# Low half of the embedding summed once and kept on both row halves: keys, queries and values with half-row products, tokens a step later

## What is computed

```
h = einsum('bnk,dk->bnd', patches(x), W)
q, k, v = silu(h @ Wq), silu(h @ Wk), silu(h @ Wv)        # 12 heads of 16
out = einsum(einsum(q, k) * decay, v) * sigmoid(h @ Wg1 @ Wg2)
h = layernorm(h + layernorm(out @ Wo) * ln_w + ln_b)
logits = l2(slots) * scale . l2(rms_norm(h)) ; dispatch, combine = softmax over tokens, over slots
y = fc2(gelu(fc1(xn . dispatch) + b1)) + b2 ; h = layernorm(h + y . combine)
```

## Time and profile before

| | |
|---|---|
| median of 3 runs | 1220.85 us (1219.61 to 1221.07) |
| profiled execution | 1220.71 us |
| its span, first to last instruction | 1219.0 us |
| mean granted TensorE clock over the span | 0.958 |
| busy, share of the span: TensorE, VectorE, ScalarE, GpSimd | 91%, 65%, 62%, 49% |

### The profile page before, as it was taken

The page is one execution under the profiler, slowest core; times in us unless marked ns, Lnnn a source line. Parts: engine busy times, 40 slices in busy tenths (PEclk is TensorE's granted clock), DMA queues, the critical chain, the costliest instruction groups (busy, mean ns, idle before and its releaser), DMA issues.

```text
span 1219.0 us, 35974 instructions
## 1 busy us (share of the span) xinstructions
PE 1105.5 (91%) x13418; PEld 889.2 (73%) x13418; DVE 787.8 (65%) x2082; ACT 750.0 (62%) x1745; POOL 595.9 (49%) x942
## 2 busy tenths in 40 slices
PE   4899999999999999999999999999998999997563
PEld 3787888888888888888888888788886556564332
DVE  5577766677777777676777777777774222222996
ACT  5567677777777776777777777776763111110676
POOL 3366655565555666555655555665533000000664
PEclk9999999999999999999999999999999999998555
DMA  4411121111111111211111111112063999995786
GB/s 151 197 51 55 58 84 59 62 53 53 53 53 53 53 53 55 80 66 61 55 53 53 53 53 53 53 53 77 32 263 129 368 424 423 424 423 181 235 264 183
DMA packets 50718, 158.41 MB, mean 130 GB/s; under 512 B 5386, under 2 KB 31392, under 8 KB 38372
## 3 DMA queue, kind: packets, MB, share of 16 engines
q1 hardware_dynamic: 33080, 145.09, 32.2%
q10 hardware_dynamic: 17600, 12.78, 3.4%
HBM read 132.23 MB, written 25.62 MB: 129 GB/s over the span
## 4 chain that ended last, share of the span: by engine, by line
PE 71%; DVE 22%; issue 2%; ACT 1%; DVEq 1%; SPq 1%; DMA 1%; POOL 0%; ACTq 0%; POOLq 0%
DVE p_sb L828 9%; PE ps L974 8%; PE ps L976 7%; PE ps L975 7%; PE ps L1271 6%; PE ps L1052 5%; PE ps L1089 4%; PE ps L1290 4%; PE ps L1134 4%; DVE gn L803 3%; PE ps L1031 3%; PE ps L1032 3%; PE ps L1019 2%; PE ps L1157 2%; DVE res L943 2%
## 5 line engine op out<-in xcount | busy, mean ns | idle before, releaser
L427 POOL TENSOR_TENSOR xl<-x_sb,xh 128x392 fp32r<-128x392 f32 x192 | 189.8, 1026 | 84.1 <-DVE gn L803 74.9
L828 DVE TENSOR_TENSOR p_sb<-ps,dec 98x1568 f32<-98x1568 f32 x96 | 171.6, 1788 | 14.8 <-PE ps L1052 14.8
L678 ACT ACTIVATE hg<-ps 128x768 f32<-128x768 f32 x32 | 25.9, 810 | 146.0 <-PE ps L1295 146.0
L768 DVE BATCH_NORM_STATS2 st<-ps 98x6 f32<-98x192 f32 x128 | 40.0, 354 | 77.5 <-PE ps L1019 77.5
L935 DVE COPY y2st<-ps 128x192 f32<-128x192 f32 x32 | 11.4, 358 | 120.5 <-PE ps L1271 120.5
L695 ACT ACTIVATE o_sb<-res,nb,rstd 98x192 f32<-98x192 f32 x128 | 59.5, 535 | 44.8 <-DVE nb L958 44.1
L1089 PE MATMUL ps<-p_sb,vpad 98*32 98x98 f32 x3072 | 84.9, 250 | 1.6 <-DVE p_sb L828 1.6
L1319 PE MATMUL ps<-y2b,cbuf 64*98 64x192 f32 x256 | 49.3, 537 | 38.1 <-POOL y2b L532 38.1
L1089 PEld LDWEIGHTS ps<-p_sb,vpad 98*32 98x32 f32 x3072 | 64.1, 109 | 26.7 <-issue 26.2
L519 POOL CAST pickb<-pick 128x128 fp32r (+1 forms) x32 | 9.4, 293 | 148.8 <-PE ps L1295 148.8
L974 PE MATMUL ps<-xl,wh 128*128 128x392 f32 x192 | 70.1, 365 | 13.1 <-POOL xl L427 13.1
(11 more groups left out here) (203 smaller groups left out, 3484.8 us busy)
## 6 DMA issues: line engine op xcount, KB each, us to landing
x_sb<-in_xT SPq DMA_DIRECT2D x32, 1176.0 KB, 5.2
w1v<-in_fc SPq DMA_DIRECT2D x32, 1152.0 KB, 10.2
w2v<-in_fc SPq DMA_DIRECT2D x32, 1152.0 KB, 12.7
h_dram<-h SPq DMA_DIRECT2D x32, 294.0 KB
h2r<-h_dram SPq DMA_DIRECT2D x32, 294.0 KB
out<-o_sb ACTq DMA_DIRECT2D x32, 294.0 KB
comb_dram<-cst SPq DMA_DIRECT2D x32, 98.0 KB, 1.7
cbuf<-comb_dram SPq DMA_DIRECT2D x32, 98.0 KB, 3.8
```

The lines of the kernel that those rows point to most:

```text
L427: pool.tensor_tensor(xl[:, k], x_sb[:, k], xh[:, k].bitcast(F32), ALU.subtract)\
L828: dve.tensor_tensor(dst, src, rate.unsqueeze(2).to_broadcast([T, 4, 2, TOK]), ALU.mult)\
```

## The change

The two partial sums of the last 64 features are added once. ScalarE copies the low part from partitions 64 to 127 into `kA[0:64]` (semaphore `hlo_sb`), VectorE adds it to the high part twice, into partitions 0 to 63 and 64 to 127 of `hT[:, 1]` (`summed_h`, `hx_rdy`), and ScalarE and VectorE make the high and low parts of that as before. The second contraction of queries, keys and values is then over 64 rows: `project` writes both output groups in turns, group 0 with rows 0 to 63 and group 1 with rows 64 to 127. Keys come first, in banks 2 and 3, then queries in banks 0 and 1; the values of the first image stand in banks 4 and 5, one half of the tokens on each row half; those of the second image in bank 7, all on rows 0 to 63. The turned embedding takes four matmuls of 64 rows instead of four of 128.

Around it the order changes on every engine. VectorE makes the tokens of pair i - 2 at the start of step i (before: of pair i - 1 in front of the first decay), the token norms between first norm and residual of the second tiles, the cosine scales behind the second statistics, the cosines in front of the `zs` subtraction, and the slots' maximum behind the second decay. ScalarE makes the squares in front of the new copy and into a buffer of their own, loads the SiLU table behind `hTh`, rounds the pixels in two places, and takes keys before queries. TensorE moves the gate behind the turned keys, the turned logits (now two transposes) in front of the third scores, and the last values in front of the slots' inputs. Output weights and slot rows are prepared at the end of step 0 instead of before it.

```diff
-V_AT = (2, 7)
+K_AT, Q_AT, V_AT = 2, 0, (4, 7)
...
-            sp.wait_ge(k_mm, 2)
+            sp.wait_ge(slT_sb, 1)
...
             def step(i, a, c, d, d_before, more):
-                if d:
-                    inverse_norms(i - 2)
...
+                if d:
+                    inverse_norms(i - 2)
...
                 if more:
-                    if c:
-                        pool.wait_ge(gn_rdy, 4 * i)
                     split_x(i + 1, range(KP))
+                if at_start(i):
...
+                if not (isinstance(j, int) and j == 0):
+                    pool.wait_ge(cosc_rdy, j)
...
+                pool.wait_ge(gn_rdy, 4 * j + 4)
...
-                if d:
+                if d and a:
                     second_norm(i - 2)
                 if a:
-                    turned_h(i, 0)
+                    turned_h(i)
                 if d:
                     act.wait_ge(tokT_mm, i - 1)
                     act.activation(tokT[:, :, :], ps[0:G, 6:8, 0:PT], ACT.Copy).then_inc(tokT_sb, 1)
-                if a:
+                    if a or c:
+                        squares(i - 2)
+                    if not a:
+                        second_norm(i - 2)
+                if a:
+                    act.wait_ge(hT_mm, 2 * i + 2)
+                    act.activation(kA[0:64, :], ps[64:128, 1, 0:PT], ACT.Copy).then_inc(hlo_sb, 1)
+                    act.wait_ge(hx_rdy, 2 * i + 2)
+                    act.activation(hTh[:, 1], hT[:, 1], ACT.Copy).then_inc(hTh_rdy, 1)
                     use_table(ACT.Silu)
-                    turned_h(i, 1)
-                if more:
-                    for k in range(2):
-                        round_x(i + 1, k)
-                if a:
+                    if more:
+                        round_x(i + 1, 0)
+                    act.wait_ge(k_mm, 2 * i + 1)
+                    act.activation(kA[:, :], ps[:, K_AT, 0:PT], ACT.Silu).then_inc(k_sb, 1)
+                    act.wait_ge(k_mm, 2 * i + 2)
...
                     act.wait_ge(q_mm, 2 * i + 1)
...
+                    act.wait_ge(v_mm, 2 * i + 1)
+                    act.activation(vpad[:, 0:2].rearrange("p t (j q d) -> p t j q d", q=4, d=HD)[:, :, :, 0:4:3, :],
...
                     act.wait_ge(q_mm, 2 * i + 2)
...
-                    act.wait_ge(k_mm, 2 * i + 1)
-                    act.activation(kA[:, :], ps[:, 0, 0:PT], ACT.Silu).then_inc(k_sb, 1)
-                    act.wait_ge(k_mm, 2 * i + 2)
...
+                    act.wait_ge(v_mm, 2 * i + 2)
+                    act.activation(vpad[:, 2:4].rearrange("p t (j q d) -> p (t j) q d", q=4, d=HD)[:, :, 0:4:3, :],
...
+                    if more:
+                        round_x(i + 1, 1)
                     if c:
                         act.wait_ge(og_sb, 2 * i)
                     act.wait_ge(g_mm, 2 * i + 1)
...
-                    turned_v(i, 1)
-                if c:
...
+                elif c:
+                    squares(i - 1)
                 if d:
                     use_table(ACT.Exp)
                     exponentials(i - 2)
...
+            def squares(j):
+                for t in range(4):
+                    act.wait_ge(gn_rdy, 4 * j + t + 1)
+                    act.activation(ysq[:, t], gn[0:T, t], ACT.Square, accum_out=ss[:, t:t + 1]).then_inc(ss_rdy, 1)
...
+            def mean_shifts(j):
+                dve.wait_ge(ra_rdy, j + 1)
...
+            def summed_h(i):
+                dve.wait_ge(hlo_sb, i + 1)
+                for x in range(2):
+                    dve.tensor_tensor(hT[64 * x:64 * x + 64, 1], ps[0:64, 1, 0:PT], kA[0:64, :],
+                                      ALU.add)                        .then_inc(hx_rdy, 1)
...
-                    token_norms(i - 2)
+                    mean_shifts(i - 2)
                 if c:
                     for g, n in enumerate((slice(0, PT), slice(PT, COLS))):
                         dve.wait_ge(ogh_rdy, 2 * i - 1 + g)
                         dve.tensor_tensor(ogl[:, n], og[:, n], ogh[:, n].bitcast(F32), ALU.subtract)\
                             .then_inc(ogl_rdy, 1)
+                if d and (a or c):
+                    tokens(i - 2)
+                if c:
                     first_norm(i - 1, 0)
                     residual(i - 1, 0)
+                if a:
+                    summed_h(i)
+                if c:
                     residual_statistics(i - 1, 0)
                 if a:
                     dve.wait_ge(hTh_rdy, 2 * i + 2)
...
                 if c:
                     first_norm(i - 1, 1)
                 if d:
-                    cosine_scales(i - 2)
+                    token_norms(i - 2)
                 if c:
                     residual(i - 1, 1)
                     residual_statistics(i - 1, 1)
+                if d:
+                    cosine_scales(i - 2)
                 if a:
                     if c:
                         dve.wait_ge(t2_rdy, 4 * i)
...
-                    dve.wait_ge(q_sb, 2 * i + 2)
-                    dve.tensor_tensor(zs[ZL:ZL + RANK, :], ps[DB:DB + RANK, 1, 0:PT], zs[0:RANK, :].bitcast(F32),
+                if d:
+                    cosines(i - 2)
+                if a:
+                    dve.wait_ge(zh_rdy, 2 * i + 2)
+                    dve.tensor_tensor(zs[ZL:ZL + RANK, :], ps[DB:DB + RANK, Q_AT + 1, 0:PT], zs[0:RANK, :].bitcast(F32),
                                       ALU.subtract).then_inc(zl_rdy, 1)
-                if d:
-                    cosines(i - 2)
-                if c:
+                if c and not a:
                     tokens(i - 1)
                 if d and not a:
                     slot_maxima(i - 2)
...
+                    decay(i, 1)
                     if d:
                         slot_maxima(i - 2)
-                    decay(i, 1)
                     dve.wait_ge(s_mm, i + 1)
...
                     sums(i - 2)
                 if a:
                     decay(i, 2)
+                    if at_start(i):
+                        output_weights()
                     gated(i, 0)
                     gated(i, 1)
+                    if at_start(i):
+                        slot_rows()
...
-            def project(i, g, hi, lo, done, more=0):
-
-                m = slice(0, DA) if g == 0 else slice(DA, D + more)
-                for k in range(2):
-                    pe.wait_ge(hTl_rdy[k], i + 1)
-                    mm = product(ps[0:m.stop - m.start, g, 0:PT], hi[:, k, m], lo[:, k, m], hTh[:, k], hTl[:, k],
-                                 k == 0, k == 1)
-                mm.then_inc(done, 1)
+            def project(i, bank, hi, lo, done, more=0):
+                groups = (slice(0, DA), slice(DA, D + more))
+                pe.wait_ge(hTl_rdy[0], i + 1)
+                for g, m in enumerate(groups):
+                    product(ps[0:m.stop - m.start, bank + g, 0:PT], hi[:, 0, m], lo[:, 0, m], hTh[:, 0], hTl[:, 0],
+                            True, False)
+                pe.wait_ge(hTl_rdy[1], i + 1)
+                for w, h in ((hi, hTl), (lo, hTh), (hi, hTh)):
+                    for g, m in enumerate(groups):
+                        rows = slice(64 * g, 64 * g + 64)
+                        mm = pe.matmul(ps[0:m.stop - m.start, bank + g, 0:PT], w[rows, 1, m], h[rows, 1],
+                                       start=False, stop=(w is hi and h is hTh))
+                        if w is hi and h is hTh:
+                            mm.then_inc(done, 1)
 
             def rows_of_v(i, a):
-                for t in (2 * a, 2 * a + 1):
-                    for k in range(2):
-                        n = slice(t * T, (t + 1) * T)
-                        mm = product(ps[0:T, V_AT[a], (t % 2) * D:(t % 2) * D + D],
-                                     hTh[:, k, n], hTl[:, k, n], wvh[:, k], wvl[:, k], k == 0, k == 1)
+                def at(mt):
+                    return ps[0:T, V_AT[0] + mt, 0:D] if a == 0 else ps[0:T, V_AT[1], mt * D:(mt + 1) * D]
+
+                def whole(mt):
+                    n = slice((2 * a + mt) * T, (2 * a + mt + 1) * T)
+                    product(at(mt), hTh[:, 0, n], hTl[:, 0, n], wvh[:, 0], wvl[:, 0], True, False)
+
+                def half(mt, h, w):
+                    x, n = mt if a == 0 else 0, (2 * a + mt) * T
+                    rows = slice(64 * x, 64 * x + 64)
+                    return pe.matmul(at(mt), h[rows, 1, n:n + T], w[rows, 1],
+                                     start=False, stop=(h is hTh and w is wvh))
+                pairs = ((hTh, wvl), (hTl, wvh), (hTh, wvh))
+                if a == 0:
+                    for mt in range(2):
+                        whole(mt)
+                    for h, w in pairs:
+                        for mt in range(2):
+                            mm = half(mt, h, w)
+                else:
+                    for mt in range(2):
+                        whole(mt)
+                        for h, w in pairs:
+                            mm = half(mt, h, w)
```

(80 more changed lines are left out.)

112 lines of the change are left out of this document (55 added, 57 removed).

## The result

The median is 1285.35 us (four runs, 1284.54 to 1286.91) against 1220.96 beside it: ratio 1.053, 95% interval 1.0512 to 1.0548, so +64.4 us. The profiled execution has a span of 1281.6 us.

The account below looks back on a forecast made before the run. TensorE was fullest (26.91 of 28 us a step), VectorE's chain nearly as long. VectorE's terms, 1.59 - 0.82 + 0.7 + 0.2 = +1.67 us over 30 steps, add 50 to 1220.7: 1271 us, range 1230 to 1291.

Parts of the forecast that it names:

- statistics to `hb`: VectorE's stretch with two added sums (1.05), the copy waited for (0.36) and moved norms and scales: +1.59 us a step.
- `Lt` to first decay: VectorE's tokens (1.32) leave this stretch and the `zs` subtraction (0.5) takes their place: net -0.82 us a step.
- second to third decay: The late maximum delays ScalarE's exponentials, for which VectorE's sums wait: 3.56 us instead of 2.84, +0.7 a step.
- third decay to next statistics: TensorE's last values wait for the decay and the slots' inputs follow: 4.5 us instead of 4.28, +0.2 a step.
- steps 0 and 1: The first steps, with output weights and slot rows prepared late in step 0: nothing taken, 4 us to either side.
- two last steps: The steps at the end of the loop: nothing taken, with 2 us to either side.
- The sum of -0.2: TensorE's matmul changes together: -0.2 us a step, lying in its waits and giving nothing.
- The bound of +0.6: Upper limit of TensorE's change in a step, +0.6 us, if no half-row pair gains at 392 columns.
- rival A: Faster: TensorE stays the bound and its half-row pairs come off the step, 1166 to 1214 us; chance 0.13.
- Rival B: No change: VectorE's idle 7.6 us of a step takes up the sums, 1221 us; chance 0.07.
- Rival C: Slower by less: maximum in time, copy not waited for, 0.6 us a step, 1239 us; chance 0.15.
- Rival D: Slower by more: pairs gain nothing, TensorE late, GpSimd stretches the sums, 0.6 more a step, 1289 us; chance 0.1.

Follow-up runs that it names:

- zs_first: The changed kernel with the `zs` subtraction on VectorE in front of the cosines again; 1274.64 us, ratio 1.044.
- slots_first: The changed kernel with the slots' inputs on TensorE in front of the last values again, as before the change; 1269.32 us, ratio 1.0401.
- norm_before_tokens: The changed kernel with ScalarE's second norm of step 32 in front of the turned tokens and squares; 1281.06 us (two runs), ratio 1.0492.
- values_half_out: The changed kernel without the six half-row matmuls of the second image's values, which then lack the last 64 features; 1292.11 us, ratio 1.0583.
- before_two_sums: The kernel before the change with two 64x392 sums added on VectorE, into a buffer that nothing reads; 1275.21 us, ratio 1.0442.

## Why the prediction was right, and where it was off

The direction, the mechanism and the wide range (1230 to 1291) held: VectorE's chain became longer, TensorE's savings vanished in its waits. The forecast's own range, 1255 to 1283, did not: the 1285.35 lies 2 us above it. Its upper end is the sum of the bounds named; its lower end is not, they would give 1243. The sum was 14 us too low (+50 predicted, +63.9 in the trace). By its own steps, in us of a step, and below them in us:

| part | predicted | measured |
|---|---|---|
| statistics to `hb` | +1.59 | +1.48 |
| `hb` to `Lt` | 0 | 0 |
| `Lt` to first decay | -0.82 | -0.60 |
| first to second decay | 0 | +0.01 |
| second to third decay | +0.70 | +0.66 |
| third decay to next statistics | +0.2 | +0.40 |
| a step | +1.67 | +1.95 |
| 30 steps | +50 | +58.3 |
| steps 0 and 1 | 0 | +2.1 |
| two last steps | 0 | +3.5 |

**The sums** were the main term and right in size: two of 0.57 us (1.05 taken, 1.15 measured), with 0.20 waited for the copy (0.36 taken); the two misses partly cancel. The run with the sums alone has +1.83 of the 1.95, without any change of TensorE's work. Its figure holds 0.41 of a slower residual, which the kernel after doesn't have in that place (0.75 at 414.29), and the parts don't simply add up: undoing the order of sums, slots' inputs or `zs` gave back 0.67, 0.59 and 0.39, and by the rows the tokens' move is on the other side.

**Between `Lt` and the first decay** the term was mis-sized by 0.22. The subtraction takes 0.60 from its start to the decay's, where I took 0.5, and it starts 0.46 behind `Lc` where the tokens started 0.34 behind it. The subtraction stood behind the cosines in the new order, beside a wait of 1.69 us that would have covered it; zs_first shows its price, 0.39.

**Behind the third decay** the term was half of what it is: +0.40. I moved the 0.80 of the slots' inputs behind the last values and added a handover, and didn't see that `ysb`'s copy loses its cover with them. slots_first gained 0.21 more than I had counted for the order, the same size.

**The two last steps** were "2 for the two last steps", as a bound to either side of nothing. They cost 3.5. In step 32 ScalarE has the second norm behind the copy of the tokens and the squares, and VectorE's first norm waits 4.07 us for it. I had read the steady step only; norm_before_tokens moves that one instruction group, and these steps become 2.85 shorter. The 0.6 that is left is open.

**Steps 0 and 1** cost 2.1, within the 4 allowed for. Step 0 is 1.07 longer although its granted clock is higher, 0.94 instead of 0.89. Step 1 has a granted clock of 0.95 where it was 1.00 before, in these rows of the windows of the kernel after and of norm_before_tokens:

```profile
45.94:72.53 26.59, 24.00 (x312) 19.51 (x311) 16.72 (x38) 11.26 (x24) 11.14 (x18) 0.95 0.50 203
```

```profile
45.90:73.70 27.80, 25.21 (x313) 20.74 (x311) 16.71 (x38) 11.26 (x24) 11.03 (x18) 0.90 0.48 195
```

Of these two the one with the lower clock is longer. How much of the 2.1 is the clock and how much the work was not separated.

**TensorE.** Keys and queries became shorter by 0.28 and 0.24 (to 2.00 and 1.99 us), 0.52 where 0.54 was taken; the second values longer by 0.68 (from 1.08 to 1.76) where 0.54 was taken. The sum of -0.2 did not come: TensorE is busy for 27.39 us of the step from 401.61 instead of 26.7, by ends that are modelled, against 26.87 before. The bound of +0.6 for "no pair gains" doesn't follow from its terms either, -0.2 and the 0.54 given back are +0.3. The wait for `hb` is 0.32 where 0.9 was forecast, and the wait of 0.26 for the sums was not forecast at all. From the last full matmul at 412.38 through three pairs to the next full one at 413.38 it is 1.00; four starts by 0.18 would be 0.72, so going into half rows and out costs 0.28, the 0.27 taken from the output projection. The Trainium skill, TensorEngine Tiling (Array Packing), Key Properties, says that a change of mode drains the array, and these rows agree. Of the doubling that the Trainium skill allows on that page, in the section Theoretical Speedup, the three pairs show 1.08 against 0.82, a factor of 1.3, with the switch in it. Nothing of it reached the time: rival A fell, as TensorE waits for VectorE five times in a step, and values_half_out takes 1.14 us out of TensorE's work in a step and leaves 25 of 30 steps as long as they were.

Rival B (the idle time of VectorE takes up the sums) fell with before_two_sums, where 1.83 of it is on the path. Rival C expected the maximum in time and the copy not waited for; both were late. Rival D gave 1289, nearer to the result than my 1271, but for reasons that didn't come: the pairs did gain, 0.28 and 0.24, the two sums were not stretched beyond 1.15, and TensorE's longer work lies in its waits.

## What to carry to other kernels

Where two engines take turns, saving work on one buys nothing while the other's part of the turn grows; count what the saved matmuls cost in preparation on the engine that they wait for. The slack behind one link of such a chain swallows only delays that arise after the work making the slack was released, so read from where each waiting piece is released before counting on it. The same late maximum cost 0.06 us a step in one kernel and 0.67 in the other, by the rows because another move had taken its cover (no run undoes both moves at once): cost moved steps together, at the fill and drain steps too.

## What the hardware showed that I had not expected

Less work for TensorE made steps slower. In values_half_out five steps had 31.3 us between steps of 29.9 (the windows, one for each step; the granted clock is the third number from the end):

```profile
102.53:133.80 31.27, 29.30 (x353) 23.05 (x349) 21.66 (x54) 20.61 (x49) 16.27 (x24) 0.89 0.16 53
133.80:163.74 29.94, 26.45 (x349) 20.95 (x349) 21.50 (x54) 20.81 (x49) 16.29 (x24) 1.00 0.16 54
163.74:195.05 31.31, 29.25 (x349) 22.96 (x349) 21.67 (x54) 20.83 (x49) 16.28 (x24) 0.89 0.15 51
195.05:224.97 29.92, 26.44 (x351) 20.94 (x349) 21.49 (x54) 20.82 (x49) 16.28 (x24) 1.00 0.15 53
```

In the long steps the granted clock has a mean of 0.89. With the levels 1.00 and 0.50 (2.4 and 1.2 GHz) this is 6.9 us at the lower one (0.11 x 31.3 / 0.5). In the steps around, TensorE was busy 26.4 of 29.9 us, with its longest wait grown to 1.14 us; in the kernel after it was busy 27.4 and the clock stayed at 1.00 in the steady steps. Five times 1.4 us is 7.0, close to the 6.8 us by which this kernel is slower than the kernel after. In windows of 2 us of the step from 163.74 the granted clock is 1.00 until 185, 0.73 from 185 to 187, 0.50 from 187 to 191, 0.56 from 191 to 193, and 1.00 behind. The wait of 1.14 us ends at 184.48, so the clock falls behind it, with TensorE at work again; but the step from 133.80 has the same wait, and its clock stays at 1.00. Why these five steps and not the others is open.

In before_two_sums the second residual (98x192, two instructions) took 1.16 us instead of 0.75. GpSimd's copy of the queries ran from 411.64 to 412.25, beside its first instruction; in the kernel before, GpSimd stood idle at that place. The first residual, of the same size, takes 1.15 in both kernels, and both times GpSimd makes `xn` beside it (412.63 to 414.76 in the kernel before). A conflict between the two engines fits, and was not tested by itself.
